# A product of k with the cosines computed on GpSimd instead of VectorE, in a four-layer kernel

## The chip, the cores and the metric

One core of one Trainium2 chip. The metric is the device time of one execution in microseconds (us), the median over the runs. Engines: TensorE (PE in the profile), VectorE (DVE), ScalarE (ACT), GpSimd (POOL), and SyncE, which issues DMAs. All run their own instruction streams and meet at semaphores. Each engine works off its stream in order.

## The reference, cut to what matters

Four layers follow each other on x of 8 batches x 256 tokens x 256 features: causal attention, a ternary linear layer, a linear attention layer and a gated feed-forward layer. The third is touched here:

```python
def rope(t, rot_dim):            # t: [B, S, D], the first rot_dim = 128 features are rotated
    ...
    t_rot, t_pass = (t[..., :rot_dim], t[..., rot_dim:])
    x = t_rot.reshape(*t_rot.shape[:-1], half, 2)
    rh = jnp.stack([-x[..., 1], x[..., 0]], axis=-1).reshape(t_rot.shape)
    t_rot = t_rot * cos + rh * sin
    return jnp.concatenate([t_rot, t_pass], axis=-1)

def feature_map(x):
    norm = jnp.sqrt(jnp.sum(x * x, axis=-1, keepdims=True))
    return x / jnp.maximum(norm, 1e-12)

QKV = jnp.einsum('bsd,ed->bse', X, W_in) + b_in     # X is the layernorm of x
Q, K, V = jnp.split(QKV, 3, axis=-1)
Q = rope(Q, rot_dim)
K = rope(K, rot_dim)
A = jnp.sum(feature_map(K) * V, axis=-2)
Y = A[:, None, :] * Q
Y = jnp.einsum('bsd,ed->bse', Y, W_out) + b_out
```

The change concerns `t_rot * cos` for K: for each batch one product of 128 partitions x 256 elements (two token tiles of 128 features).

## The kernel before

The program order of each engine is written out by hand. The attention layer takes most of the time: batch by batch, with eight steps j of two heads each; the ternary layer of the batch before is worked into it. The linear attention layer then runs in the **linear stage**, from about 440 to 495 us of the span, and the gated layer behind it to the end.

The linear stage is a software pipeline over passes n = 1 to 7, each engine with its own function `linear(n)`; batch 0's part of k stands in the last step of the attention. In pass n (from 2 on) the engines do this, in order:

- TensorE: k's projection of batch n (L647, needs the low part of x's transpose, `linear_x_lo`), the token sums of batch n - 1 (L926, `linear_sum`: rotated k against weighted x; needs k_rotate of n - 1), the transposes of batch n + 1 (L657), the output projection of n - 2 (L938), q's projection of n. In pass 7 the transposes are those of the gated layer's first two batches.
- VectorE: normalises batch n + 1 (`linear_apply`, L1770), q's products of n - 1 (L1800, L1803), copies k out of PSUM with its bias (`k_copy`, L1783), multiplies it with the cosines (`k_cosine`, L1791), finishes the sums of n - 1 (L1815), makes the low part of x of n + 1 (`linear_x_lo`, L1508, after ScalarE's high part), and adds the output (`linear_add`, L1758). Single passes have more: in 2 and 5 the low part of the down weights (`down_weights_lo`, L1859), in 7 the gated layer's low part (L1892) and its normalisation of batch 1 (`gated_apply(1)`, L1883). In pass 1 the order is another: sums, `linear_x_lo(2)`, then `k_cosine(1)`, then the ternary layer's statistics.
- ScalarE: residual, the squares of k (`k_squares`, L1346, after `k_copy`), the high part of x of n + 1 (L1112; L1295 for the gated layer), y, the weighing of x with the inverse norms (`weigh`, after k_inverse), a copy of q.
- GpSimd: q's rotation of n - 1 (`q_rotate`, L489, after q's products), `k_sine` (L472, two half products, after `k_copy`), `k_inverse` (L508, L512: inverse norms, after the squares), `k_rotate` (L482: sum of both products, in place in k, after `k_sine`, `k_cosine` and the squares). Then in single passes: in 2 `ternary_bias(7)` (L459, 512 elements), in 3 and 4 `linear_scale`, in 5 a quarter of the gate and up weights' low part (L538, 352 elements), in 6 inverse deviations.

The products lie in buffers by the parity of n: `k_cos[q]` and `k_sin[q]`, q = n % 2. Waits go by counting semaphores: `s_lke` counts k_copy, `s_lkc` the cosine products, `s_lr` k_rotate.

Of the kernel before, what the change touches and what calls it, by code (L numbers as in the profile page):

```python
# [18 lines left out]
ALU = mybir.AluOpType  # L19
# [3 lines left out]
P = 128  # L23
# [23 lines left out]
def build(nc, x_in, wk_in, wv_in, wq_in, wp_in, wt_in, gb_in, bias_in, bin_in, win_in, wout_in, wgu_in, sgu_in,  # L47
          wd_in, rope_in, out):
    with ExitStack() as ctx:
# [73 lines left out]
        k_sb = [qkv[:, q, :, D:2 * D] for q in range(2)]  # L123
        k_cos = [qkv[:, q, 0, 2 * D:3 * D].rearrange("p (t e i) -> p t e i", t=ST, e=2) for q in range(2)]
# [26 lines left out]
        rope = sb("rope", [P, 2, ST, 2, P])  # L151
# [110 lines left out]
        s_lke = sem("linear_k_copied")  # L262
        s_lsq = sem("k_norm_squared")
        s_lkc = sem("k_cosine_products")
# [162 lines left out]
        def _(pool):  # L427
# [37 lines left out]
            def k_sine(n):  # L465
# [6 lines left out]
                    m = pool.tensor_tensor(k_sin[q][:, :, e, :], k[:, :, 1 - e, :], sin[:, :, e, :], ALU.mult)  # L472
                m.then_inc(s_lks, 1)

            def k_rotate(n):

                q = n % 2
                k = k_sb[q][:, :, 0:P].rearrange("p t (e i) -> p t e i", e=2)
                pool.wait_ge(s_lks, n + 1)
                pool.wait_ge(s_lkc, n + 1)  # L480
                pool.wait_ge(s_lsq, n + 1)
                pool.tensor_tensor(k, k_cos[q], k_sin[q], ALU.add).then_inc(s_lr, 1)  # L482
# [107 lines left out]
            def linear(n):  # L590
                if n > 0:
                    q_rotate(n - 1)
                k_sine(n)
                k_inverse(n)
                k_rotate(n)
                if n == 1:
                    inv_std_twice(NB - 1)
                if n == NB - 2:
                    inv_std(NB)
                if n == 2:  # L600
                    ternary_bias(NB - 1)
                if n == 3:
                    linear_scale(NB - 2)
                if n == 4:
                    linear_scale(NB - 1)
                if n == 5:
                    pool.wait_ge(s_ln, NB - 1)
                    gated_weights_lo(GU1, 3)
                if n == NB - 2:
                    gated_inv_std()  # L610
# [873 lines left out]
        def _(dve):  # L1484
# [112 lines left out]
            def batch(n, last):  # L1597
                for j in range(J):
                    first = isinstance(n, int) and n == 0 and j == 0
                    if not (isinstance(n, int) and n == 0 and j < 2):  # L1600
                        pT_lo(n, j, 0)
                        pT_lo(n, j, 1)
                    opening = isinstance(n, int) and n == 0 and j < 5
                    if first:
                        v_lo(n, 1)
                    if opening and not first:
                        normalise(n, j + 1)
                    if first:
                        row_max_rest(n, 2)
                        q_lo(n, 3)  # L1610
                    elif j < J - 2 or not last:
                        row_max(*ahead(n, j, 2))
                        if not opening:
                            normalise(*ahead(n, j, 1))
                    if first:
                        o_lo(n, 0)
                        pT_lo(n, 1, 0)
                        pT_lo(n, 1, 1)
                        invert_sums(n, 2)
                    if j == 0 and not first:  # L1620
                        v_lo(n, 1)
                    if j in (5, 6) and not last:
                        k_lo(n + 1, j - 5)
                    if not first and (j < J - 3 or not last):
                        q_lo(*ahead(n, j, 3))
                    if not (isinstance(n, int) and n == 0):
                        if j == 1:
                            ternary_apply(n - 1)
                        if j == 2:
                            ternary_lo(n - 1)  # L1630
                        if j == 3:
                            add_bank(n - 1, bM, s_fp, s_fb, s_fa)
                    if j == 4:
                        linear_x_lo(0, 0) if last else x_lo(n + 1)

                    if j == 0 and not (isinstance(n, int) and n == 0):
                        ternary_moments(n - 1)
                    if j == 2 and not last:
                        if isinstance(n, int):
                            dve.wait_ge(s_x[n + 1], 16)  # L1640
                        ln_moments(n + 1, n + 1)
                    if j == 3 and not last:
                        x_apply(n + 1)
                    if isinstance(n, int) and n == 0 and j > 3:
                        ternary_weights(j - 3)
                    if j == 2 and isinstance(n, int) and n == 0:
                        ternary_weights(0)
                        pick_q_bias()
                    if j == J - 1 and not (isinstance(n, int) and n == 0) and not last:
                        linear_moments(n - 1)  # L1650
                    if last:
                        if j == 3:
                            linear_apply(0)
                        if j == 1:
                            pick_v_bias()
                        if j == 5:
                            linear_apply(1)
                            o_lo(n, j)
                        if j == 6:
                            invert_sums(n, J - 1)  # L1660
                            normalise(n, J - 1)
                            q_products(0)
                            o_lo(n, j)
                            linear_x_lo(1, 1)
                            linear_moments(NB - 2)
                    if j == J - 1 and last:
                        k_copy(0)
                        k_cosine(0)
                    if j == J - 1:
                        o_lo(n, j)  # L1670
                    if (j < J - 3 or not last) and not first:
                        invert_sums(*ahead(n, j, 2))
                    if (j < J - 3 or j < J - 1 and not last) and not first:
                        o_lo(n, j)
                if not last:
                    v_lo(n + 1, 0)
                    add_y(n)
# [105 lines left out]
                dve.tensor_tensor(k_sb[n % 2], bK[n % 2][:, :].rearrange("p (t d) -> p t d", t=ST),  # L1783
                                  b_k.rearrange("p (o d) -> p o d", o=1).to_broadcast([P, ST, D]), ALU.add).then_inc(s_lke, 1)

            def k_cosine(n):
                q = n % 2
                dve.wait_ge(s_lke, n + 1)
                k = k_sb[q][:, :, 0:P].rearrange("p t (e i) -> p t e i", e=2)
                cos = rope[:, 0, :, 0, :].rearrange("p t (i e) -> p t e i", e=2)  # L1790
                dve.tensor_tensor(k_cos[q], k, cos, ALU.mult).then_inc(s_lkc, 1)  # L1791

            def q_products(n):
                dve.wait_ge(s_lqe, n + 1)
                if n == 0:
# [22 lines left out]
            def linear(n):  # L1818
                if n > 1:
                    linear_apply(n + 1) if n + 1 < NB else gated_apply(0)  # L1820
                    q_products(n - 1)
                    if n == 2:
                        ternary_apply(NB - 1)
                    if n == 3:
                        ternary_lo(NB - 1)
                    k_copy(n)
                    k_cosine(n)
                    linear_sum(n - 1)
                    if n < NB - 1:
                        linear_x_lo(n + 1, (n + 1) % 2)  # L1830
                    else:
                        gated_x_lo(0)
                        gated_apply(1)
                    linear_add(n - 2)
                else:
                    linear_sum(n - 1)
                    linear_x_lo(n + 1, (n + 1) % 2)
                    k_cosine(n)
                    ternary_moments(NB - 1)
                if n == 2:  # L1840
                    down_weights_lo(0, 3 * D, DOWN0)
                if n == 3:
                    add_bank(NB - 1, bO, s_fp, s_fb, s_fa)
                if n == 4:
                    linear_moments(NB - 1)
                if n == 5:
                    down_weights_lo(3 * D, HT * D, DOWN1)
                if n == NB - 2:
                    ln_moments(NB, 0)
                    gated_moments()  # L1850
                if n == NB - 1:
                    dve.wait_ge(s_lop, 1)
                    dve.tensor_reduce(lo_sum[:, :], bO[:, 8:12], AX.X, ALU.add).then_inc(s_lor, 1)
                    dve.wait_ge(s_lor, 1)
                    dve.tensor_scalar(lo_flag[:, :], lo_sum[:, :], 0.0, None, ALU.is_gt).then_inc(s_flag, 1)
# [250 lines left out]
```

## Time and profile before

| | us |
|---|---|
| median of 3 runs | 572.52 (572.25 to 573.15) |
| the profiled execution | 572.94 |
| its span, first to last instruction | 571.1 |
| busy: TensorE, VectorE, ScalarE, GpSimd | 560.6, 464.1, 370.5, 210.9 |
| granted TensorE clock | 0.999 of full speed |

The profile records one execution. "Busy" is the time in which an engine had an instruction running; names are the program's, with the line of the code. A timeline merges neighbours of one line and operation, and says in brackets how long the engine stood idle before an instruction, and for what.

### The profile page before, as it was taken

To read this page: it belongs to the slowest core of one execution; us is meant where nothing else is said; L and a number is where in the kernel's file an instruction comes from. 1 tells how busy PE (TensorE), PEld (TensorE's weight loads), DVE (VectorE), ACT (ScalarE), POOL (GpSimd) and SP (SyncE) were. 2 spreads that over 40 slices of the span, in tenths; PEclk is the share of its full clock that TensorE was granted. 3 is DMA by queue.
4 is the path that set the end of the run, shared out by engine and by line. 5 is a ranking of instruction groups with operands and counts; after the bars stand their busy time and mean duration, and the time that the engine had idled before them with its cause. 6 is when DMAs were issued, how large, how long until landed. Compare 5 with 4: busy or idle time off the path is not lost.

```text
span 571.1 us, 12867 instructions
## 1 busy us (share of the span) xinstructions
PE 560.6 (98%) x4135; PEld 530.1 (93%) x4135; DVE 464.1 (81%) x1475; ACT 370.5 (65%) x1037; POOL 210.9 (37%) x316
## 2 busy tenths in 40 slices
PE   8999999999999999999999999999999999999996
PEld 8899999999999999999999999999998899888885
DVE  4888789778977997798789778977887899878875
ACT  5887556656755756666657566756985777754553
POOL 3782224233223332342234223223356677413221
PEclk9999999999999999999999999999999999999999
DMA  8807000000000000000000000000000000001002
GB/s 329 299 1 231 2 1 3 1 1 0 0 0 0 0 0 0 0 0 0 0 0 0 0 0 0 0 0 1 2 1 1 1 2 1 1 1 38 15 23 77
DMA packets 9152, 14.71 MB, mean 26 GB/s; under 512 B 1568, under 2 KB 6688, under 8 KB 9120
## 3 DMA queue, kind: packets, MB, share of 16 engines
q1 hardware_dynamic: 8848, 14.04, 7.0%
q8 instruction: 18, 0.29, 0.2%
q10 hardware_dynamic: 272, 0.26, 0.1%
q14 instruction: 14, 0.11, 0.1%
HBM read 12.20 MB, written 2.10 MB: 25 GB/s over the span
## 4 chain that ended last, share of the span: by engine, by line
PE 91%; DVE 4%; ACT 3%; issue 1%; POOL 0%; DVEq 0%; POOLq 0%
PE bank L647 71%; PE bank L750 5%; PE bank L732 3%; PE bank L657 2%; PE bank L753 2%; PE bank L938 2%; PE bank L926 2%; PE bank L863 1%; PE bank L734 1%; ACT prob L1150 1%; PE bank L1057 1%; ACT big L1123 0%; DVE prob L1562 0%; DVE qT L1508 0%; ACT raw L1346 0%
## 5 line engine op out<-in xcount | busy, mean ns | idle before, releaser
L521 POOL TENSOR_SCALAR prob<-prob,rowinv 128x256 f32<-128x256 f32 (+1 forms) x127 | 96.3, 770 | 267.2 <-DVE rowinv L1578 267.2
L647 PE MATMUL bank<-xT,big 128*128 128x256 f32 x984 | 129.5, 283 | 0.1
L647 PEld LDWEIGHTS bank<-xT,big 128*128 128x128 f32 x984 | 123.2, 191 | 1.0 <-issue 0.2
L1150 ACT ACTIVATE prob<-prob,negmax 128x128 f32<-128x128 f32 (+1 forms) x256 | 112.8, 445 | 8.4 <-DVE negmax L1562 8.4
L647 PE MATMUL bank<-wp,oT 128*128 128x256 f32 x768 | 102.5, 283 | 0.4 <-DVE oT L1508 0.3
L647 PEld LDWEIGHTS bank<-wp,oT 128*128 128x128 f32 x768 | 96.8, 190 | 1.4 <-DVE oT L1508 0.8
L1112 ACT ACTIVATE qT<-bank 128x512 fp32r<-128x512 f32 x68 | 40.6, 597 | 71.5 <-PE bank L647 71.4
L647 PE MATMUL bank<-pT,v 128*128 128x512 f32 (+1 forms) x384 | 79.8, 343 | 0.7 <-DVE pT L1508 0.5
L647 PEld LDWEIGHTS bank<-pT,v 128*128 128x128 f32 x384 | 63.2, 189 | 9.9 <-issue 1.0
L1508 DVE TENSOR_TENSOR pT<-bank,pT 128x512 fp32r<-128x512 f32 (+1 forms) x128 | 65.1, 550 | 3.0 <-ACT pT L1112 2.9
L1112 ACT ACTIVATE pT<-bank 128x512 fp32r<-128x512 f32 (+1 forms) x128 | 55.2, 483 | 13.1 <-PE bank L750 11.0
L1508 DVE TENSOR_TENSOR qT<-bank,qT 128x512 fp32r<-128x512 f32 x68 | 46.7, 687 | 16.6 <-ACT qT L1112 16.5
L647 PE MATMUL bank<-kT,qT 128*128 128x256 f32 x384 | 59.4, 290 | 0.0
L1508 DVE TENSOR_TENSOR oT<-bank,oT 128x512 fp32r<-128x512 f32 x64 | 44.0, 688 | 15.8 <-ACT oT L1112 15.0
L647 PEld LDWEIGHTS bank<-kT,qT 128*128 128x128 f32 x384 | 49.5, 189 | 0.0
L1150 ACT ACTIVATION_READ_ACCUMULATOR prob<-prob,negmax 128x1 f32 x256 | 48.7, 190 | 0.0
L1562 DVE CUSTOM_DVE_ANT_0 prob<-bank,mask 128x256 f32<-128x256 f32 x128 | 48.6, 416 | 0.0
L647 PE MATMUL bank<-wp,big 128*128 128x512 f32 (+2 forms) x180 | 45.4, 394 | 0.1
L1112 ACT ACTIVATE oT<-bank 128x512 fp32r<-128x512 f32 x64 | 37.3, 582 | 4.3 <-PE bank L647 4.3
L750 PE MATMUL bank<-ident,prob 128*128 128x128 f32 x256 | 38.4, 272 | 0.0
L732 PE MATMUL bank<-kT,qT 128*128 128x256 f32 x128 | 38.0, 348 | 0.4 <-DVE qT L1508 0.3
L647 PEld LDWEIGHTS bank<-wp,big 128*128 128x128 f32 x180 | 32.0, 189 | 5.9 <-issue 0.3
(189 smaller groups left out, 990.5 us busy)
## 6 DMA issues: line engine op xcount, KB each, us to landing
raw<-in_wq SPq DMA_DIRECT2D x4, 512.0 KB, 6.5
raw<-in_wp SPq DMA_DIRECT2D x4, 512.0 KB, 6.9
x<-in_x SPq DMA_DIRECT2D x7, 256.0 KB, 6.8
out<-x SPq DMA_DIRECT2D x6, 256.0 KB, 2.1
raw<-in_w_gu SPq DMA_DIRECT2D x2, 640.0 KB, 5.4
raw<-in_w_in SPq DMA_DIRECT2D x1, 768.0 KB, 4.8
raw<-in_w_down SPq DMA_DIRECT2D x1, 640.0 KB, 7.3
raw<-in_wk SPq DMA_DIRECT2D x1, 512.0 KB, 3.9
```

The source lines that it names most:

```text
L521: m = pool.tensor_scalar(prob[:, j % 2, 0, a:b], prob[:, j % 2, 0, a:b], rowinv[:, j % 2, r:r + 1], None, ALU.mult)
L647: m = pe.matmul(out, lhs(a), rhs(b), start=first and i == 0, stop=last and i == len(passes) - 1, skip_group_check=True)
L657: m = pe.transpose(out[:, k * S + t * P:k * S + (t + 1) * P], src[:, t, k * P:(k + 1) * P], ident[:])
L732: pe.matmul(bS0[:, i * S:(i + 1) * S], qT[:, 0, i, 0:P], kT[:, :, g, 0:P], start=True, stop=False, skip_group_check=True)
L750: m = pe.transpose(bT0[:, i * S + r * P:i * S + (r + 1) * P], prob[:, j % 2, i, r * P:(r + 1) * P], ident[:])
L753: m = pe.transpose(bT1[:, i * P:(i + 1) * P], prob[:, j % 2, i, 2 * P:3 * P], ident[:])
L926: m = pe.matmul(bA[e][:, 0:D + 1], k_sb[n % 2][:, t, e * P:(e + 1) * P], xw[n % 2][:, t, :], start=t == 0, stop=t == ST - 1)
L938: m = pe.matmul(bY[:, t * D:(t + 1) * D], yT[:, k, t * P:(t + 1) * P], lin_out[:, k, :], start=False, stop=t + k == 2, skip_group_check=True)
L1112: act.activation(out, src, ACT.Copy).then_inc(done, 1)
L1150: m = act.activation(prob[:, j % 2, i, a:b], prob[:, j % 2, i, a:b], ACT.Exp, scale=-1.0, bias=negmax[:, 2 * i + r:2 * i + r + 1], accum_o ...
L1508: dve.tensor_tensor(out, src, f32(hi), ALU.subtract).then_inc(done, 1)
L1562: return dve.tensor_tensor_reduce(prob[:, j % 2, i, a:b], src, other, -SCALE, -MASKED, ALU.add, ALU.min, negmax[:, 2 * i + r:2 * i + r + 1])
```

## The change

GpSimd gets its own `k_cosine(n)`, without a wait of its own, since `k_sine(n)` has just waited for `k_copy(n)`. It is called between `k_inverse(n)` and `k_rotate(n)` in all eight passes. VectorE's function and its three calls go; the one for batch 0 stood in the attention's last step. The semaphore `s_lkc` remains: k_rotate now waits with it for GpSimd's own instruction. Operands, result and buffers are the same.

```diff
+            def k_cosine(n):
+                q = n % 2
+                k = k_sb[q][:, :, 0:P].rearrange("p t (e i) -> p t e i", e=2)
+                cos = rope[:, 0, :, 0, :].rearrange("p t (i e) -> p t e i", e=2)
+                pool.tensor_tensor(k_cos[q], k, cos, ALU.mult).then_inc(s_lkc, 1)
+
             def k_rotate(n):
...
                 k_sine(n)
                 k_inverse(n)
+                k_cosine(n)
                 k_rotate(n)
...
                     if j == J - 1 and last:
                         k_copy(0)
-                        k_cosine(0)
...
-            def k_cosine(n):
-                q = n % 2
-                dve.wait_ge(s_lke, n + 1)
-                k = k_sb[q][:, :, 0:P].rearrange("p t (e i) -> p t e i", e=2)
-                cos = rope[:, 0, :, 0, :].rearrange("p t (i e) -> p t e i", e=2)
-                dve.tensor_tensor(k_cos[q], k, cos, ALU.mult).then_inc(s_lkc, 1)
-
...
                     k_copy(n)
-                    k_cosine(n)
                     linear_sum(n - 1)
...
                     linear_sum(n - 1)
                     linear_x_lo(n + 1, (n + 1) % 2)
-                    k_cosine(n)
                     ternary_moments(NB - 1)
```

On GpSimd, pass 2 as it was, from q's rotation of batch 1 to the ternary bias:

```order
L489 TENSOR_TENSOR qkv<-raw 128x256
L472 TENSOR_TENSOR qkv<-qkv,rope 128x2x64 x2
L508 TENSOR_SCALAR k_bound<-k_norm 128x2
L512 TENSOR_TENSOR prob<-k_bound,exponent 128x2
L482 TENSOR_TENSOR qkv<-qkv 128x2x128
L459 TENSOR_TENSOR x<-x,biases 128x512
```

The same place of the changed program, whose lines are numbered a little higher (k_rotate is L488 there, the new product L479):

```order
L495 TENSOR_TENSOR qkv<-raw 128x256
L472 TENSOR_TENSOR qkv<-qkv,rope 128x2x64 x2
L514 TENSOR_SCALAR k_bound<-k_norm 128x2
L518 TENSOR_TENSOR prob<-k_bound,exponent 128x2
L479 TENSOR_TENSOR qkv<-qkv,rope 128x256
L488 TENSOR_TENSOR qkv<-qkv 128x2x128
L459 TENSOR_TENSOR x<-x,biases 128x512
```

k_rotate and the ternary bias stand one instruction further back. In pass 5 it is k_rotate and the weights' low part.

On VectorE, pass 2 as it was, from k's copy to the normalisation of batch 4 in the next pass:

```order
L1783 TENSOR_TENSOR qkv<-bank,b_in 128x2x256
L1791 TENSOR_TENSOR qkv<-qkv,rope 128x256
L1815 ISA prob,A_sb<-bank,linear_wv_bias 128x257
L1815 ISA A_sb 128x1
L1815 ISA b_in,A_sb<-bank,linear_wv_bias 128x257
L1815 ISA A_sb 128x1
L1508 TENSOR_TENSOR qT<-bank,qT 128x512
L1758 TENSOR_TENSOR x<-bank,biases 128x512
L1859 SCALAR_TENSOR_TENSOR big<-raw,big 128x768
L1770 TENSOR_SCALAR xn<-x,linear_negated_mean,linear_rstd 128x256 x2
```

And now:

```order
L1789 TENSOR_TENSOR qkv<-bank,b_in 128x2x256
L1814 ISA prob,A_sb<-bank,linear_wv_bias 128x257
L1814 ISA A_sb 128x1
L1814 ISA b_in,A_sb<-bank,linear_wv_bias 128x257
L1814 ISA A_sb 128x1
L1515 TENSOR_TENSOR qT<-bank,qT 128x512
L1764 TENSOR_TENSOR x<-bank,biases 128x512
L1856 SCALAR_TENSOR_TENSOR big<-raw,big 128x768
L1776 TENSOR_SCALAR xn<-x,linear_negated_mean,linear_rstd 128x256 x2
```

The cosine product in the second row is gone, and nothing else has moved.

## Rows read from the trace of the kernel before

**Rows 1.** The page: the span, and busy time with its share by engine.

```profile
span 571.1 us, 12867 instructions
...
PE 560.6 (98%) x4135; PEld 530.1 (93%) x4135; DVE 464.1 (81%) x1475; ACT 370.5 (65%) x1037; POOL 210.9 (37%) x316
```

**Rows 2.** TensorE's waits, 435 to 500 us: total us, times, longest us.

```profile
PE bank L657 <- DVE xn L1883: 1.1, 1, 1.1
```

**Rows 3.** The chain of waits near the linear stage's end: start us, us, what.

```profile
481.28 1.62 PE bank L938 x8
...
488.55 0.70 DVE qkv L1783
...
489.28 0.84 ACT raw L1346 x4
490.12 0.56 ACT wp L1295
...
491.31 1.14 DVE xn L1883 x2
...
492.50 0.66 PE bank L657 x4
```

**Rows 4.** TensorE's timeline: start us, us, engine, line, operation, names, shapes, count.

```profile
457.28 1.90 PE L926 MATMUL bank<-prob,qkv 128*128 128x257 f32 x8
...
463.87 1.59 PE L647 MATMUL bank<-big,xT 128*128 128x256 f32 x12
```

**Rows 5.** VectorE's timeline, same columns; in brackets idle time before, and releaser.

```profile
448.02 0.42 DVE L1791 TENSOR_TENSOR qkv<-qkv,rope 128x256 f32<-128x256 f32 x1
...
454.99 0.69 DVE L1508 TENSOR_TENSOR qT<-bank,qT 128x512 fp32r<-128x512 f32 x1 [0.31 <-ACT qT L1112]
...
456.20 1.05 DVE L1859 SCALAR_TENSOR_TENSOR big<-raw,big 128x768 fp32r<-128x768 int32 x1
457.17 1.68 DVE L1770 TENSOR_SCALAR xn<-x,linear_negated_mean,linear_rstd 128x256 f32<-128x256 f32 x2
...
463.02 0.69 DVE L1508 TENSOR_TENSOR xT<-bank,xT 128x512 fp32r<-128x512 f32 x1 [0.31 <-ACT xT L1112]
...
476.92 1.15 DVE L1859 SCALAR_TENSOR_TENSOR big<-raw,big 128x768 fp32r<-128x768 int32 x1
478.17 1.19 DVE L1770 TENSOR_SCALAR xn_b<-x,linear_negated_mean,linear_rstd 128x256 f32<-128x256 f32 x2
```

**Rows 6.** The removed product: duration ns min/median/max, first and last start us.

```profile
L1791 DVE TENSOR_TENSOR qkv<-qkv,rope x8: 416/425/427, 440.7 to 489.3; 128x256 f32<-128x256 f32 x8
```

**Rows 7.** GpSimd's timeline, columns as in rows 5.

```profile
444.36 0.98 POOL L472 TENSOR_TENSOR qkv<-qkv,rope 128x128 f32<-128x128 f32 x2
...
453.61 1.14 POOL L472 TENSOR_TENSOR qkv<-qkv,rope 128x128 f32<-128x128 f32 x2 [1.15 <-DVE qkv L1783]
...
455.69 0.74 POOL L482 TENSOR_TENSOR qkv<-qkv 128x256 f32<-128x256 f32 x1
456.39 1.99 POOL L459 TENSOR_TENSOR x<-x,biases 128x512 f32<-128x512 f32 x1
...
476.51 0.74 POOL L482 TENSOR_TENSOR qkv<-qkv 128x256 f32<-128x256 f32 x1
477.21 1.67 POOL L538 TENSOR_TENSOR big<-raw,big 128x352 fp32r<-128x352 f32 x1
...
491.51 0.78 POOL L482 TENSOR_TENSOR qkv<-qkv 128x256 f32<-128x256 f32 x1
```

**Rows 8.** Three lines of the code in their own views, columns as in rows 6.

```profile
L1770 DVE TENSOR_SCALAR xn<-x,linear_negated_mean,linear_rstd x8: 404/412/1357, 419.1 to 471.7; 128x256 f32<-128x256 f32 x8
...
L459 POOL TENSOR_TENSOR x<-x,biases x8: 1292/1302/1986, 87.6 to 456.4; 128x512 f32 x6, 128x512 f32<-128x512 f32 x2
...
L538 POOL TENSOR_TENSOR big<-raw,big x8: 937/948/1667, 428.1 to 477.2; 128x352 fp32r<-128x352 f32 x8
```

## The prediction, made before the changed kernel ran

> **What bounds the kernel now.** I read the page first. TensorE is busy for 98% of a span of 571.1 us [rows 1], so an edit on VectorE or GpSimd matters only where it makes TensorE wait or takes a wait away. Then I asked for TensorE's waits in the linear stage, 435 to 500 us: one is as long as 1 us, 1.1 us for VectorE's last normalisation (L1883) in front of the transposes L657 [rows 2]. The chain of waits shows what stands behind it [rows 3]: TensorE runs to 482.90, and from there the chain is VectorE's. It passes through k's copy (L1783, 488.55), ScalarE's squares of k (L1346), ScalarE's high part (L1295), VectorE's L1883, and is back on TensorE at 492.50. So for the last passes VectorE with ScalarE is a loop of its own, late against TensorE, and what it gains or loses arrives at 492.50 one for one. Until the last pass TensorE waits for it hardly at all, but the margin is small: k's projection of batch 4 starts at 463.87 [rows 4], and the low part that it needs is done at 463.02 + 0.69 = 463.71 [rows 5].
>
> The third view is VectorE's timeline. Between 448.02 and 454.99 it has no idle time; at 454.99 it waited 0.31 us for ScalarE [rows 5]. That gap returns in each pass n from 2 on, for k's copy lets ScalarE square k and then make the high part, on which VectorE's low part waits. The removed product stands just behind the copy, in that shadow.
>
> **The change, part by part.**
>
> *Removed from VectorE:* eight products of 0.42 us [rows 6]. Instructions in a row overlap by 0.08 us (L1859 ends at 456.20 + 1.05 = 457.25, the next starts at 457.17 [rows 5]), so each is worth 0.34 us where VectorE is the bound. In passes 2 to 7 it is hidden: the wait for ScalarE merely grows from 0.31 to 0.65 us. For batch 0 it stands inside the same shadow, in front of a wait for ScalarE: nothing. Only in pass 1 the product stands behind the low part (448.02) with VectorE full after it. Gain: 0.34 us once, from pass 2 on.
>
> *Added to GpSimd:* eight products of 128x256 elements. Its nearest row is k_rotate (L482, two SBUF inputs, same size): 0.74 us, the next one starting 0.70 us after [rows 7]. The strided operands are like those of k_sine, 0.49 us for each half product when alone (0.98 the two at 444.36 [rows 7]); bounds 0.70 and 0.98, and I take 0.70, because a fixed part is paid once and not twice. It delays k_rotate and all of GpSimd's instructions behind it. k_inverse stays ahead of it, so ScalarE's weighing isn't later. On the other hand k_sine no longer runs beside VectorE's product: 1.14 us at 453.61 against 0.98 at 444.36, where none ran [rows 7], gives 0.14 to 0.16 back.
>
> *k_rotate and the token sums.* Net, k_rotate comes 0.70 - 0.15 = 0.55 us later against k's copy. In pass 2 it ended at 456.43 and TensorE's token sums (L926) start at 457.28 [rows 4, 7], with 0.85 us of room; other passes have more or about the same. In pass 1 k_rotate even starts earlier, since it no longer waits for VectorE's 448.02. Cost by itself: nothing, but the room is used up.
>
> *What the longer GpSimd row meets.* Some instructions of the two engines don't run side by side. L459 takes 1.30 us as a rule and 1.99 in pass 2, behind VectorE's L1859; L1770 takes 0.41 as a rule and 1.357 then; L538 takes 0.95 as a rule and 1.67 behind the second L1859 [rows 7, 8]. The sums fit one owner at a time. L459 was held 1.99 - 1.30 = 0.69 us, so it began in effect at 456.39 + 0.69 = 457.08, close to L1859's end; L1770 was held 1.357 - 0.41 = 0.95, until 457.17 + 0.95 = 458.12, that is 1.04 us after L459's real start. So L459 owns the resource for 1.04 us, its duration less some 0.2, hence a 0.74 us product for 0.55. L1859 was free at about 455.69 + 0.55 = 456.24 and gave way at 457.08: 0.84 us. The Trainium skill ("SBUF — State Buffer", section "Who interferes with whom") says the same: a VectorE instruction with two SBUF inputs, or a tensor_scalar in its two-port mode, and a GpSimd instruction exclude each other, and the later one fully blocks. The rows above agree, and by that rule the edit takes one excluded instruction off VectorE and puts another, longer one on GpSimd.
>
> Now the three places.
>
> Pass 2. VectorE is 0.34 early: L1859 arrives at 455.86. GpSimd's product starts at 455.69 - 0.34 - 0.14 = 455.21, k_rotate arrives at 455.91. It is a near tie. If L1859 wins: it owns 455.86 to 456.70, k_rotate to 457.25 (done at 457.44), the first L1770 runs 457.25 to 457.65, L459 owns 457.5 to 458.54, the second L1770 ends at 458.94, against 457.17 + 1.68 = 458.85 before: +0.1. If k_rotate wins: it owns to 456.48, L1859 to 457.32, L459 to 458.36, the L1770s end at 459.1: +0.25. So the gain of 0.34 is gone and the loop is 0.1 to 0.25 late. In the first order TensorE's sums also wait some 0.2 us at 457.28, but these are made good, as TensorE is ahead of the loop in the end.
>
> Pass 5. Product from about 476.51 - 0.15 = 476.36 to 477.1, L1859 arrives at 476.92 and k_rotate at 477.06: a near tie again. L1859 first: owned to 477.76, k_rotate to 478.31, first L1770 to 478.6, L538 (owns about 0.73) to 479.3, second L1770 ends near 479.7 against 478.17 + 1.19 = 479.36 before: +0.33. k_rotate first: 477.6, L1859 to 478.4, L538 to 479.1, both L1770 to 479.87: +0.5. All of it shifts with the delay of pass 2.
>
> Pass 7. Product arrives at 491.51 - 0.15 = 491.36, the first L1883 at 491.31 [rows 3, 7]. L1883 first: the second one is held until 492.11, +0.07. Product first: both are held, and k_rotate gets between them, up to +0.65.
>
> Sum: 0.1 to 0.25, plus 0.33 to 0.5, plus 0.07 to 0.65: 0.5 to 1.4 us. I take 0.17 + 0.43 + 0.1 = 0.7 us, with the last place at its lower end because L1883 is there first by these numbers.
>
> Beside it GpSimd is simply slower: 0.74 us for what took 0.42 [rows 6, 7]. The Trainium skill ("GPSIMD Engine Reference", section "4.1 Engine selection") puts elementwise work with two inputs on VectorE, GpSimd being about twice as slow; the ratio of the rows is 1.8, and the rule alone would make it 0.84 us, 0.1 more on GpSimd per pass.
>
> The profiled execution took 572.94 us, for its span of 571.1; the median shown is 572.52. Profiled: 573.6. Median: 573.2, which is +0.13%.
>
> **The rivals.**
>
> *A: gain, small.* The resource matters less than I say, or the ties fall well, and the 0.34 us of pass 1 survive to 492.50, or are just used up. For it: until 454.99 nothing is in the way. Against it: L1770 was already held 0.95 us in pass 2, so an earlier VectorE only waits longer. Time: 572.2 to 572.5.
>
> *B: clearly slower.* The place is pass 7: if VectorE's L1883 arrives just after GpSimd's product, both halves are held in turn, +0.65. With passes 2 and 5 at their upper ends the loop is 1.4 late. It decides once the product is issued before the first L1883, for which 0.05 us is missing by my numbers. If GpSimd's product also costs the upper 0.98, three collisions grow by 0.28 each and k_rotate misses the token sums: +2. Time: 573.8 to 574.5.
>
> *C: nothing.* The product on VectorE was in ScalarE's shadow, and GpSimd is busy for only 37% of the span [rows 1]; the held instructions only swap places. Time: 572.5. GpSimd's idle time speaks for it, the near ties against.
>
> **How the numbers follow.** My forecast (+0.45 to +1.0) has 0.48, A 0.12, B 0.20, C 0.18, 0.02 for others. The range of 572.1 to 574.1 reaches from A, less a little for the scatter of the runs (572.25 to 573.15), into B, and leaves out 0.1 above and little below. A change within 0.2%, 1.1 us, is about what can't be told from none: my forecast, A and C lie within it. Of B three quarters are beyond, of the forecast a small part. Faster 0.02, same 0.80, slower 0.18. A gain of 1.1 us has no source: VectorE gives up 0.34 us on the path.
>
> **What would show it.** GpSimd's new line near 0.74 us, and k_sine near 0.98. The idle time before the low part near 0.65. In pass 2 the second L1770, done at 458.85 before, done at 458.9 to 459.1. In pass 5 one or both L1770 held for 0.5 us or more. TensorE's wait in front of the last transposes, 1.1 us, longer by most of the loss. I am wrong if L1770 and L1859 run undisturbed beside the new product, if the wait at L657 shrinks, or if TensorE waits for k_rotate by more than 0.3 us in several passes.

## The result and the profile after

The changed kernel takes 573.75 us (median of 14 runs, 572.62 to 575.32), the kernel before 572.52 us (14 runs, 571.97 to 573.15): ratio 1.0024, 95% interval 1.0017 to 1.003. It is slower by 1.2 us, just past the 0.2% that can be told from no change. The profiled execution took 574.82 us.

The page of the changed kernel, with the rows that answer to [rows 1]:

```profile
span 572.9 us, 12867 instructions
...
PE 561.3 (98%) x4135; PEld 530.6 (93%) x4135; DVE 462.4 (81%) x1467; ACT 370.3 (65%) x1037; POOL 215.2 (38%) x324
```

GpSimd has 4.3 us more and VectorE 1.7 us less. VectorE's removed products were 3.4 us [rows 6], so it got back only half: its other instructions grew. TensorE's waits from 435 to 500 us, beside [rows 2]:

```profile
PE bank L664 <- DVE xn L1880: 1.9, 1, 1.9
...
PE bank L933 <- issue: 0.3, 1, 0.3
```

The wait in front of the last transposes (L664 here) grew from 1.08 to 1.85 us, and there is a new one, 0.35 us in front of token sums in pass 2 (L933, "issue": nothing that the view can name; k_rotate, which they need, is done at 457.15, 0.10 us before they start). TensorE's timeline at both places:

```profile
442.51 1.69 PE L654 MATMUL bank<-wp,oT 128*128 128x256 f32 x12 [0.27 <-DVE oT L1515]
...
454.87 0.60 PE L664 MATMUL bank<-ident,y 128*128 128x128 f32 x4
455.23 1.67 PE L654 MATMUL bank<-big,qT 128*128 128x256 f32 x12
457.25 1.98 PE L933 MATMUL bank<-prob,qkv 128*128 128x257 f32 x8 [0.35 <-issue]
...
493.00 0.66 PE L664 MATMUL bank<-ident,xn 128*128 128x128 f32 x4 [1.85 <-DVE xn L1880]
493.50 3.40 PE L933 MATMUL bank<-prob,qkv 128*128 128x257 f32 x8
```

The same places of the kernel before, with two more rows for later use:

```profile
442.88 1.69 PE L647 MATMUL bank<-wp,oT 128*128 128x256 f32 x12 [0.27 <-DVE oT L1508]
...
455.13 0.60 PE L657 MATMUL bank<-ident,y 128*128 128x128 f32 x4
455.74 1.70 PE L647 MATMUL bank<-big,qT 128*128 128x256 f32 x12
...
492.50 0.66 PE L657 MATMUL bank<-ident,xn 128*128 128x128 f32 x4 [1.08 <-DVE xn L1883]
```

The last row of the changed kernel has eight matmuls that took 3.40 us; those of pass 2, the same form, took 1.98 us. The windows tell why (columns: us, TensorE, its weight loads, VectorE, ScalarE, GpSimd busy, granted clock, DMA share, GB/s):

```profile
492.00:494.00 2.00, 1.00 (x6) 0.97 (x7) 1.77 (x5) 0.91 (x3) 0.72 (x1) 0.93 0.00 0
494.00:496.00 2.00, 2.00 (x6) 1.54 (x6) 0.75 (x2) 1.98 (x4) 0.00 (x0) 0.50 0.00 0
496.00:498.00 2.00, 2.00 (x9) 1.62 (x7) 1.33 (x6) 0.52 (x1) 0.00 (x0) 0.72 0.00 0
498.00:500.00 2.00, 2.00 (x10) 1.70 (x9) 1.95 (x5) 0.23 (x1) 0.74 (x1) 1.00 0.01 4
```

Behind the wait the granted clock is at 0.50, the lower of TensorE's two levels (1.2 GHz). The means 0.93 and 0.72 of the windows in which it falls and rises put that at about 493.7 to 497.1 us. The kernel before shows 1.00 in the same windows:

```profile
492.00:494.00 2.00, 1.50 (x9) 1.39 (x10) 1.27 (x4) 1.71 (x5) 0.30 (x1) 1.00 0.00 0
494.00:496.00 2.00, 2.00 (x11) 1.76 (x10) 1.25 (x4) 1.98 (x3) 0.00 (x0) 1.00 0.00 0
496.00:498.00 2.00, 2.00 (x10) 1.68 (x10) 1.94 (x6) 0.43 (x2) 0.41 (x1) 1.00 0.00 0
```

VectorE, beside [rows 5] (L1515 was L1508, L1856 was L1859, L1776 was L1770, L1880 was L1883):

```profile
454.40 0.69 DVE L1515 TENSOR_TENSOR qT<-bank,qT 128x512 fp32r<-128x512 f32 x1 [0.77 <-ACT qT L1119]
...
455.61 0.95 DVE L1856 SCALAR_TENSOR_TENSOR big<-raw,big 128x768 fp32r<-128x768 int32 x1
456.48 2.11 DVE L1776 TENSOR_SCALAR xn<-x,linear_negated_mean,linear_rstd 128x256 f32<-128x256 f32 x2
...
476.62 0.95 DVE L1856 SCALAR_TENSOR_TENSOR big<-raw,big 128x768 fp32r<-128x768 int32 x1
477.87 1.41 DVE L1776 TENSOR_SCALAR xn_b<-x,linear_negated_mean,linear_rstd 128x256 f32<-128x256 f32 x2 [0.30 <-ACT prob L1360]
...
491.24 1.71 DVE L1880 TENSOR_SCALAR xn<-x,ternary_moments,ternary_rstd 128x256 f32<-128x256 f32 x2
```

GpSimd, beside [rows 7] (L479 is the new product, L488 k_rotate):

```profile
453.02 0.89 POOL L472 TENSOR_TENSOR qkv<-qkv,rope 128x128 f32<-128x128 f32 x2 [1.15 <-DVE qkv L1789]
...
454.95 0.75 POOL L479 TENSOR_TENSOR qkv<-qkv,rope 128x256 f32<-128x256 f32 x1
455.83 1.32 POOL L488 TENSOR_TENSOR qkv<-qkv 128x256 f32<-128x256 f32 x1
457.11 1.32 POOL L459 TENSOR_TENSOR x<-x,biases 128x512 f32<-128x512 f32 x1
...
476.88 1.29 POOL L488 TENSOR_TENSOR qkv<-qkv 128x256 f32<-128x256 f32 x1
478.13 0.99 POOL L544 TENSOR_TENSOR big<-raw,big 128x352 fp32r<-128x352 f32 x1
...
491.20 0.74 POOL L479 TENSOR_TENSOR qkv<-qkv,rope 128x256 f32<-128x256 f32 x1
492.08 0.72 POOL L488 TENSOR_TENSOR qkv<-qkv 128x256 f32<-128x256 f32 x1
```

The two profiles reach the same work at slightly different times, so I read distances. The distance from TensorE's matmul after its wait near 443 us (row 442.51 here, 442.88 in the kernel before) to the start of the last transposes I call the **stretch**; it leaves out the start and the tail of the execution, which differ by some tenths of a us between most profiles, and once by 1.2 us. Before it is 492.50 - 442.88 = 49.62 us, after 493.00 - 442.51 = 50.49 us: +0.87. A longer one, **to the end**, runs to the start of VectorE's last row (566.64 before, 568.57 after) and takes in what comes behind the wait: 123.76 and 126.06 us, +2.30. The difference, 1.43 us, is the low clock's.

In the VectorE rows one sees where the 0.87 came from. In pass 2 the pair L1776, the two normalisations of a batch, took 2.11 us (1.68 before) but had started earlier, and was done at 458.59, 16.08 after 442.51, where it was at 15.97 before: +0.11. In pass 5 the pair took 1.41 instead of 1.19, and by L1880 VectorE is at 48.73 against 48.43: +0.30 in all. In pass 7 the pair L1880 took 1.71 instead of 1.14: +0.57 more. GpSimd's product had started at 491.20, 0.04 us ahead of it, so that both halves were held (columns as in [rows 6]; 0.41 us each is the undisturbed size [rows 8]):

```profile
L1880 DVE TENSOR_SCALAR xn<-x,ternary_moments,ternary_rstd x2: 853/894/935, 491.2 to 492.0; 128x256 f32<-128x256 f32 x2
```

### The profile page after: what moved, and what is told of

Read it like the earlier page. It is cut to its first block, busy times and chain, and to the rows that moved or that the text cites. A ratio compares the mean times of both kernels' runs of the same rounds, so it can differ in the third digit from the quotient of the medians.

```text
span 572.9 us, 12867 instructions
## 1 busy us (share of the span) xinstructions
PE 561.3 (98%) x4135; PEld 530.6 (93%) x4135; DVE 462.4 (81%) x1467; ACT 370.3 (65%) x1037; POOL 215.2 (38%) x324
## 4 chain that ended last, share of the span: by engine, by line
PE 90%; DVE 4%; ACT 3%; DMA 1%; issue 1%; SPq 1%; POOL 0%; DVEq 0%
PE bank L654 70%; PE bank L757 5%; PE bank L739 3%; PE bank L933 2%; PE bank L664 2%; PE bank L760 2%; PE bank L945 2%; PE bank L870 1%; DMA raw<-in_wp 1%; PE bank L741 1%; ACT prob L1157 1%; DVE prob L1569 0%; DVE qT L1515 0%; ACT raw L1353 0%; DVE xn L1880 0%
## 5 line engine op out<-in xcount | busy, mean ns | idle before, releaser
L1515 DVE TENSOR_TENSOR pT<-bank,pT 128x512 fp32r<-128x512 f32 (+1 forms) x128 | 65.2, 551 | 3.0 <-ACT pT L1119 2.9
L1515 DVE TENSOR_TENSOR qT<-bank,qT 128x512 fp32r<-128x512 f32 x68 | 46.7, 687 | 17.9 <-ACT qT L1119 17.8
L1515 DVE TENSOR_TENSOR oT<-bank,oT 128x512 fp32r<-128x512 f32 x64 | 44.1, 689 | 16.2 <-ACT oT L1119 15.5
```

Of the source, the lines that this page charges most:

```text
L1515: dve.tensor_tensor(out, src, f32(hi), ALU.subtract).then_inc(done, 1)
```

## The experiments

Each ran on a chip beside runs of the kernel before (22 to 34 executions). "Stretch" and "to the end" are the two distances above, as differences to the profile of before (the expectations of before_same_wait, after_filled_again, pass5_7_on_vector and early_product_pass7 say "stretch" for the longer one, to the end); "wait" is TensorE's in front of the last transposes; "pair" is VectorE's normalisation ahead of them; all from one profile each. Medians are given as differences to the median of before on the same chip. They hold every execution, two odd ones with them: 1411 us in before_delay2 and 1786 us in before_long_delay_filled; without these the two medians are 0.03 and 0.08 us lower.

| kernel | wait | pair | stretch | to the end | median | ratio, 95% interval |
|---|---|---|---|---|---|---|
| before | 1.08 | 1.14 | 0 | 0 | 0 | |
| changed | 1.85 | 1.71 | +0.87 | +2.30 | +1.23 | 1.0017 to 1.003 |
| after_again | 1.85 | 1.71 | +0.85 | +2.33 | +1.30 | 1.0011 to 1.0029 |
| pass7_on_vector | 1.28 | 1.13 | +0.24 | +0.20 | +0.18 | 0.9997 to 1.0014 |
| only_pass7_on_gpsimd | 1.68 | 1.71 | +0.62 | +0.57 | +0.29 | 0.9999 to 1.0016 |
| pass5_7_on_vector | 1.10 | 1.14 | +0.07 | +0.29 | +0.30 | 0.9996 to 1.0014 |
| before_delay2 | 1.36 | 0.74 | +0.28 | +0.34 | +0.27 | 0.9995 to 1.0012 |
| before_same_wait | 1.87 | 0.72 | +0.81 | +0.74 | +0.90 | 1.0006 to 1.0025 |
| before_long_delay | 2.46 | 0.72 | +1.38 | +1.37 | +2.42 | 1.0029 to 1.0054 |
| before_long_delay_filled | 0.28 | 0.72 | +1.39 | +1.38 | +2.61 | 1.0031 to 1.0057 |
| after_filled | 0.55 | 1.72 | +0.87 | +0.86 | +0.84 | 1.001 to 1.003 |
| after_filled_again | 0.53 | 1.71 | +0.84 | +0.86 | +0.84 | 1.0003 to 1.0021 |
| early_product | 0.62 | 0.73 | +0.69 | +1.25 | +1.16 | 1.0017 to 1.0035 |
| early_product_pass7 | 0.86 | 0.73 | -0.15 | +0.37 | +0.33 | 0.9995 to 1.0013 |

Theory 1: the loss is the meeting of GpSimd's longer row with VectorE's normalisation, in pass 7 above all, and what TensorE's longer wait brings with it. Theory 2: it is spread over the eight products.

**pass7_on_vector.** The product of pass 7 goes back to VectorE.

```diff
+        ON_VECTOR = (7,)
...
-                k_cosine(n)
+                if n not in ON_VECTOR:
+                    k_cosine(n)
                 k_rotate(n)
...
                     k_copy(n)
+                    if n in ON_VECTOR:
+                        k_cosine(n)
                     linear_sum(n - 1)
```

> The changed kernel, but in pass 7 alone the cosine product stays on VectorE as before. Theory 1 (most of the loss is pass 7: GpSimd's product is issued just before VectorE's last normalisation, both halves of it are held, TensorE waits 1.85 us and its clock falls): the pair takes 1.1 to 1.2 us again, TensorE waits 1.3 to 1.4 us, median 572.7 to 572.9, no execution at 574.7. Theory 2 (the loss is spread over the passes, each GpSimd product costing its share): seven eighths remain, 573.6.

Measured: 572.87 us, 0.18 over before, with all executions below 573.5. VectorE's timeline:

```profile
491.23 0.69 DVE L1908 TENSOR_TENSOR wp<-bank,wp 128x512 fp32r<-128x512 f32 x1 [0.31 <-ACT wp L1308]
491.84 1.13 DVE L1899 TENSOR_SCALAR xn<-x,ternary_moments,ternary_rstd 128x256 f32<-128x256 f32 x2
```

The pair takes 1.13 us again. One product in eight carries most of the loss, where theory 2 wanted 573.6; it is out.

**only_pass7_on_gpsimd.** The converse: ON_VECTOR is (0, ..., 6).

> The kernel before, but in pass 7 alone the cosine product is on GpSimd. Theory 1: TensorE waits about 1.08 + 0.5 = 1.6 us in front of the last transposes, median 573.0 to 573.3, and some executions lose another 1.4 us to the clock. Theory 2: one eighth of the loss, 572.7.

Measured: 572.98 us, +0.29; stretch +0.62. VectorE and GpSimd, in that order:

```profile
490.81 1.71 DVE L1899 TENSOR_SCALAR xn<-x,ternary_moments,ternary_rstd 128x256 f32<-128x256 f32 x2
```

```profile
490.77 0.74 POOL L481 TENSOR_TENSOR qkv<-qkv,rope 128x256 f32<-128x256 f32 x1
```

Product first by 0.04 us again, and by 0.03 to 0.04 us in all five profiles that have it there: both instructions hang on k's copy, so the order isn't left to chance. +0.24 and +0.62 add up to about the changed kernel's +0.87. The median lost less than the profile (its interval holds no change), and no execution lay above 573.6, where I had expected some.

**before_delay2.** Extra work on VectorE ahead of the pair, nothing moved on GpSimd.

```diff
                         gated_x_lo(0)
+                        for t in range(2):
+                            dve.bn_stats(l_stats[:, t % ST, :], x_tile(0, t % ST))
                         gated_apply(1)
```

> The kernel before, with two extra statistics instructions of 0.37 us each on VectorE in front of the last normalisation (their result is not used); nothing moves on GpSimd. TensorE's wait grows by 0.66 to 0.74 us to about 1.8. If a longer wait alone brings the clock down: the executions spread over 573.2 to 575 like the changed kernel's, and the profile may show 0.5 for some us after the wait. If the clock fell for another reason: all executions within 572.9 to 573.6.

Measured: 572.96 us, +0.27, and a wait of 1.36 us, not 1.8. My number for the wait was wrong for an instructive reason: 0.67 us later the pair no longer meets k_rotate and takes 0.74 us instead of 1.14. So 0.40 us of the kernel before's own wait was already such a meeting.

**before_same_wait.** Two statistics of 512 elements in the same place, for the changed kernel's wait.

```diff
                         gated_x_lo(0)
+                        for stat in (l_stats[:, 0, :], l_stats[:, 1, :]):
+                            dve.bn_stats(stat, x[:, 0:ST, :].rearrange("p t d -> p (t d)"))
                         gated_apply(1)
```

> The kernel before, with two statistics instructions of 512 elements on VectorE in front of the last normalisation (result not used), so that TensorE waits about 1.85 us as in the changed kernel, with nothing moved on GpSimd. The stretch from TensorE's first matmul after its wait at 443 to VectorE's last instruction grows by 0.75 us without a fall of the clock, by 2.2 us with one. If the length of the wait is what brings the fall: 0.5 in the windows behind the wait. If it is something else in the changed kernel (or chance, as with 2.46 us there was none in the one profile): full clock, median 573.2 to 573.5.

Measured: 573.45 us, +0.90. TensorE's timeline, and the clock behind it:

```profile
493.27 0.66 PE L657 MATMUL bank<-ident,xn 128*128 128x128 f32 x4 [1.87 <-DVE xn L1885]
```

```profile
494.00:496.00 2.00, 2.00 (x11) 1.75 (x10) 0.56 (x2) 1.98 (x4) 0.00 (x0) 1.00 0.00 0
496.00:498.00 2.00, 2.00 (x11) 1.72 (x10) 1.97 (x8) 0.78 (x1) 0.00 (x0) 1.00 0.00 0
```

Full clock behind a wait of 1.87 us. The wait costs its length and, in this profile, no more; two of 11 executions were above 574, one of them (574.33) at a mean granted clock of 0.996, the other (574.99) at full clock.

**before_long_delay** (three such statistics, the third into t_stats) and **before_long_delay_filled** (the same, with 20 transposes of the identity by TensorE inside the wait).

> The kernel before, with three statistics instructions of 512 elements (about 0.63 us each, result not used) on VectorE in front of the last normalisation. TensorE's wait grows from 1.08 to 2.5 or 2.7 us, which alone makes 574.0 to 574.3. If a long wait brings the clock down: most executions at 575.3 or more, and the profile shows 0.5 for some us behind the wait. If not: all within 573.6 to 574.8.

> The same, with 20 transposes of the identity on TensorE inside the wait, so that it stands still for some 0.4 us instead of 2.6. If standing still is what brings the clock down: full clock behind the wait in the profile, median 574.0 to 574.3, and at least 1 us less than without them. If not: as without them.

Measured: 574.95 and 575.14 us, from five and six executions. TensorE in the first:

```profile
494.00 0.66 PE L657 MATMUL bank<-ident,xn 128*128 128x128 f32 x4 [2.46 <-DVE xn L1885]
```

```profile
494.00:496.00 2.00, 2.00 (x11) 1.83 (x12) 0.77 (x3) 1.36 (x3) 0.00 (x0) 1.00 0.00 0
```

Again full clock, behind 2.46 us. In both kernels the medians are 1.0 to 1.2 us above what the profile's distances give, and the filled one is no faster, against my expectation. Part of that extra can be placed. Without the fill, two executions took 574.22 (the profiled one) and 574.24 us at a mean granted clock of 0.999, and three took 574.95 to 575.18 us at 0.994 to 0.996: these had a lower clock somewhere, and no window shows where. The profiled execution of the filled kernel took 575.57 us, and its extra lies behind the work: the span ends 5.65 us after the start of VectorE's last row, where it was 4.46 us in the kernel before. Why, stays open. So this pair doesn't test whether filling a long wait saves anything.

**after_filled** and **after_filled_again.** The changed kernel with the wait filled.

```diff
                 if n == NB - 1:
+                    pe.wait_ge(s_lke, NB - 1)
+                    for _ in range(12):
+                        pe.transpose(bS0[:, 0:P], ident[:], ident[:])
                     gated_transpose(1)
```

> The changed kernel, with 12 transposes of the identity on TensorE into a free PSUM bank in front of the last transposes, inside the wait. If the clock fell because TensorE stood still: it stays at full speed, no execution above 574.2, median 573.2 to 573.5 (about 0.8 over the kernel before). If the wait has nothing to do with it: 573.7 with the same spread.

> The changed kernel with TensorE's wait filled by 12 transposes, once more. If standing still is what brings the fall of the clock: full clock in the profile again, the stretch 0.75 to 0.9 us longer than before, median 573.3 to 573.6. If the fall is chance: 0.5 in the profile this time may be, as in both profiles of the changed kernel.

Measured: 573.53 and 573.39 us, both +0.84; one execution of the first lay at 575.65 (mean clock 0.997), where I had expected none above 574.2, and none of the second above 573.7. The second's TensorE and clock:

```profile
493.47 0.66 PE L664 MATMUL bank<-ident,xn 128*128 128x128 f32 x4 [0.53 <-DVE xn L1883]
```

```profile
494.00:496.00 2.00, 2.00 (x12) 1.76 (x11) 0.53 (x4) 1.87 (x4) 0.00 (x0) 1.00 0.00 0
```

The stretch is unchanged, for it belongs to VectorE, and the clock is full in both profiles. To the end the two are 1.44 us shorter than the changed kernel. In the medians the fill is worth only 0.4 to 0.5 us, which would mean that the clock fell in a part of the timed executions; the section below counts them by their mean clock.

**after_again.** The changed kernel on the second chip.

> The changed kernel once more, on the chip on which the next three run. Both theories: 573.4 to 573.9. If the falls of the clock belong to it, some executions lie at 574.6 or more, 2 to 5 of 11; if they were an accident of the first chip, none.

Measured: 573.83 us, 573.05 to 574.53. Its profile repeats the first one's:

```profile
494.00:496.00 2.00, 2.00 (x6) 1.54 (x6) 0.83 (x2) 1.98 (x4) 0.00 (x0) 0.50 0.00 0
```

The fall is in both profiles of the changed kernel and in none of the other twelve. But no execution reached 574.6 us, where I had expected 2 to 5 of 11. Of the ten, the profiled one alone, at 574.53, has a mean clock as low as 0.996.

**early_product** and **early_product_pass7.** GpSimd's product in front of k_inverse, in every pass and in pass 7 alone.

```diff
                 k_sine(n)
-                k_inverse(n)
-                k_cosine(n)
+                if n in (7,):
+                    k_cosine(n)
+                    k_inverse(n)
+                else:
+                    k_inverse(n)
+                    k_cosine(n)
                 k_rotate(n)
```

(In early_product the tuple is 0 to 7.)

> The changed kernel with GpSimd's product in front of k_inverse in every pass instead of behind it, so that in pass 7 it ends before VectorE's last normalisation arrives. Theory 1 (the loss is the product meeting that normalisation): the pair takes 1.1 us or less, TensorE waits 1.3 us or less, median 572.6 to 572.9. Rival (what costs is GpSimd's longer row, wherever the product stands in it; the inverse norms now come 0.75 us later, and ScalarE's weighing with them): 573.4 or more.

> The changed kernel, with GpSimd's product in front of k_inverse in pass 7 alone. Theory 1: the last normalisation isn't held (its pair takes 0.75 us), the transposes come about 1 us earlier than in the changed kernel, and the token sums then wait some 0.3 us for ScalarE's weighing, as when all passes have it; the stretch is 0.1 to 0.4 us longer than before, no fall of the clock, median 572.6 to 572.9. Rival (the later inverse norms cost as much as the collision): 573.2 or more.

Measured: 573.69 and 572.88 us. The pair takes 0.73 us in both, as theory 1 wanted. With all passes changed the kernel is as slow all the same, and there the rival was right: TensorE now waits for ScalarE's residual and weighing.

```profile
468.33 1.97 PE L949 MATMUL bank<-raw 128*128 128x256 f32 x8 [0.32 <-ACT bank L1315]
...
494.22 2.00 PE L937 MATMUL bank<-prob,qkv 128*128 128x257 f32 x8 [0.32 <-ACT prob L1364]
```

In pass 7 alone the transposes are 0.15 us earlier than before and the token sums 0.33 us later, as expected; the median is 0.33 us higher, with an interval that holds no change.

**pass5_7_on_vector.** ON_VECTOR is (5, 7).

> The changed kernel, with the products of passes 5 and 7 on VectorE as before; six of eight products stay on GpSimd. Theory 1 (of the 0.77 us in the profile, 0.20 comes from pass 5 and 0.57 from pass 7, and the others cost nothing in the end): the stretch is as before within 0.1 us, TensorE waits 1.1 us, median 572.5 to 572.7. Theory 2 (each GpSimd product costs its share): 573.2 or more.

Measured: 572.85 us, +0.30, where 572.5 to 572.7 was expected and theory 2 wanted 573.2. TensorE:

```profile
442.45 1.69 PE L660 MATMUL bank<-wp,oT 128*128 128x256 f32 x12 [0.27 <-DVE oT L1521]
...
492.14 0.66 PE L670 MATMUL bank<-ident,xn 128*128 128x128 f32 x4 [1.10 <-DVE xn L1899]
```

The stretch is as before, 49.69 us, so the six other products cost nothing there. To the end it is +0.29, not within the 0.1 that I had expected: 0.2 us is added at the very end, where TensorE's wait for the last low part was 0.52 us instead of 0.31; I haven't followed it up. The interval holds no change. None of these kernels is faster than the one before.

## Why the prediction was right where it was

**The bound and the place.** VectorE with ScalarE was the loop that ends the linear stage, and the wait in front of the last transposes took the loss: 1.85 us for 1.08. The forecast of +0.7 for this path stands against +0.87 in the profile and +0.84 in the medians of both filled kernels. That the sum came out so near is luck: of its three terms, 0.17 measured 0.11, 0.43 measured another 0.19, and 0.1 measured 0.57. The errors nearly cancelled. The measured +1.23 lies in the range, but above my forecast (+0.45 to +1.0) and just below B's 573.8, and past the 1.1 us for which "same" had 0.80; "slower" had 0.18. What is missing between +0.87 and +1.23 is the clock's, which the sum didn't have. (573.2 was +0.12% over 572.52, not +0.13%.)

**Pass 1's gain.** VectorE ran 0.22 us ahead by pass 2's low part (454.40 is 11.89 after 442.51; 454.99 [rows 5] is 12.11 after 442.88), not 0.34, since TensorE was 0.11 us late out of the token sums of batch 0. I had given those sums no cost. The wait for ScalarE in front of the low part grew to 0.77 us where I had 0.65: with the product went the gap in front of it (from copy to product 0.71 us, from the copy to what now follows 0.60), which bought nothing either. My statement that TensorE hardly waits for the loop was off too. In the kernel before, k's projection of batch 3 (455.74) came just as its low part was done (454.99 + 0.69 = 455.68 [rows 5]); with that part earlier TensorE went on at once, 455.23 after 454.87. That was a real gain of 0.25 us (12.72 us after the row at 443 instead of 12.86, although TensorE had come 0.11 us late to that place).

**Pass 2.** The near tie fell to L1859 (L1856 here), the first order of the two, by 0.22 us. k_rotate was held to 1.32 us, and TensorE's sums waited for it, 0.35 us where I had 0.2. So the gain was given back at once; three passes later, at the second L1856, TensorE stood at +0.06 and VectorE at +0.07. The step that was short: from the product to k_rotate it is 0.88 us (454.95 to 455.83), not 0.70. That spacing stands in every pass (0.87 to 0.89). k_rotate waits by semaphore for the product just ahead of it, and where the next instruction has no such wait the spacing is 0.70; no run took the wait away, so this reason is read off, not tested.

**Pass 5.** The same order again. Forecast was +0.33, and the pair grew by 0.22. With pass 2's 0.07 to 0.11 the loop came to +0.30 ahead of pass 7, where I had 0.43 to 0.75: both near ties went the cheap way, and even that order was priced 0.1 us too high.

**Pass 7, the step that failed.** I put it at 0.07 us because the product seemed to come 0.05 us too late; it came 0.04 us early and cost 0.57, the upper end that I had left to rival B. The term behind it is k_sine. I took 0.98 us for it undisturbed, from the row at 444.36 [rows 7], but that pair ran beside VectorE's L1770 and was held itself (0.51 us for each half); undisturbed it is 0.89 us (453.02). The trace of the kernel before had the right number: of the pair at 453.61 the second half, behind VectorE's product, took 0.465 us. With the decision at 0.05 us, 0.09 us in a duration changed the sign of the order. The experiments show this place: a stretch of +0.24 without it, +0.62 with it alone.

**What wasn't in the sum.** In both profiles of the changed kernel the clock fell to its lower level behind the wait, 1.43 us in the profile. It explains why the profiled execution (574.82) is so far above the median. Full clock in the profiles of both filled kernels speaks for the wait as a condition; full clock behind 1.87 and 2.46 us in the delayed ones shows that a wait of that length doesn't bring a fall each time. What decides when it falls stays open.

The timed executions have no windows, but each one's mean granted clock is known: the two profiled executions with the fall have 0.996, the twelve without it 0.997 to 1.00. The changed kernel's 14 executions fall into two groups: nine from 572.62 to 573.96 us, whose median of 573.40 (+0.88) fits the stretch's +0.87, and five from 574.69 to 575.32, with mean clocks of 0.996 three times, 0.997 and 0.948. At 0.996 or less were 5 of the 24 executions of the changed kernel on both chips, none of the 22 of the filled ones, one of 89 of the kernel before (0.948), one of 11 of before_same_wait, three of five of before_long_delay and one of six of before_long_delay_filled. So a fall doesn't seem to belong to the moved product: kernels whose long wait was made on VectorE alone had low mean clocks too. Where in those executions the clock was low, nothing shows.

**Rivals.** A is out: the early gain existed and was gone within a pass. C is out: the held instructions didn't only swap places, the last pair's 0.57 us arrived at TensorE. B had the mechanism of pass 7 right, without its upper bounds elsewhere; its decision, the product issued before the first L1883, is what happened.

## What to carry to other kernels

An instruction taken off a busy engine is worth nothing where the engine then waits for the same neighbour; look at what the freed engine waits for next before moving work to an idle one. In these traces GpSimd's products held VectorE's normalisations and its instructions with two SBUF operands, and were held by them, so a longer GpSimd row must be checked against every such VectorE instruction that it now reaches, and the last one before TensorE's longest wait counts most. Where an order is decided by less than 0.1 us, price both orders and take a duration only from a row that nothing disturbed.

## What the runs showed of the hardware

A GpSimd instruction of 128x256 with two float32 operands in SBUF took 0.74 to 0.75 us undisturbed, with strided operands (the product) as without (k_rotate). The next instruction started 0.70 us after it, or 0.88 us when it waited by semaphore for that product. The instruction that started first went first also by a margin of 0.04 us; behind it the two engines took turns: product, first half of L1880 (0.85 us for 0.41), k_rotate (0.72 us, not held), second half (0.94 us). The Trainium skill ("SBUF — State Buffer", section "Who interferes with whom") says that issue order decides who blocks; the margin of 0.04 us agrees.

TensorE's granted clock was 0.50 for some 3 us behind a wait of 1.85 us in two profiles, and 1.00 behind waits of 1.68, 1.87 and 2.46 us in three others, one each.
